# A transformer layer with routed experts: which batches are routed first, and who adds x for batch 0

## The chip, the cores and the metric

The kernel runs on one core of a Trainium2 chip. The metric is the device time of one execution in microseconds (us); less is better. A core has five engines that run side by side and meet at semaphores: TensorE (PE in the profile, PEld its weight loads), VectorE (DVE), ScalarE (ACT), GpSimd (POOL) and SyncE (SP), which here only issues DMAs. GpSimd issues the indirect DMAs, the ones whose rows are chosen by an index.

## What is computed

```python
def layer(x, ...):                                    # x: 4 batches x 512 tokens x 256, fp32
    x = x + layernorm(attention(layernorm(x)))        # 16 heads of 128, causal
    return x + layernorm(ffn(layernorm(x)))

def ffn(x):                                           # 2048 tokens
    logits = x @ router                               # 8 experts, each token goes to the best 2
    e, w = top2(logits); w = softmax(w)
    pos = rank of (token, choice) among those of its expert, in order of the tokens; kept if pos < 640
    buf[e, pos] = x[token]                            # the scatter
    out = (silu(buf @ gate) * (buf @ up)) @ down      # hidden width 176 per expert
    routed[token] += w * out[e, pos]                  # the gather
    shared = (silu(x @ sgate) * (x @ sup)) @ sdown    # hidden width 704
    return routed + shared
```

## The kernel before

Tokens stand in 16 tiles of 128 (TILES), four to a batch (TPB = 4, B = 4). Each engine has its own instruction stream, written out by hand; an engine runs its stream strictly in order, and every meeting between engines is a semaphore wait in the code. So the order of the lines in each engine's block is the schedule.

**Attention**, up to about 570 us, is a pipeline over 64 (batch, head) units. Batches 0 to 2 get their first norm, their sum with x and their second norm inside this pipeline. For batch 3 these come behind it: VectorE takes the projections back (`take_back`), normalizes them, adds x (line 1481) and takes the statistics of the sum (`stats_of_x2`, `variances`); GpSimd forms the inverse deviation (`inverse_std2`, line 1668); VectorE forms the shift (`scale_x2`); ScalarE writes the normalized tiles xn2 (`x_normed`, line 634); TensorE transposes them (`turn`, line 940).

**Routing** is done in two groups (GROUPS): group 0 is batches 0 to 2, twelve tiles, group 1 is batch 3, four tiles. For a group TensorE forms the logits (`logits`), ScalarE copies them (`logits_copied`), TensorE transposes them so that tokens stand on partitions (`turn_logits`, line 956), VectorE picks the experts (`choose`, lines 1410 to 1433), TensorE counts the positions (`positions`, lines 965 and 966), and VectorE turns them into row numbers (`find_slots`, lines 1442 to 1456; line 1454 writes at_in and frees `slots_ready`). GpSimd then issues two indirect DMAs a tile, 24 for group 0 and 8 for group 1, which scatter xn2 into slot_inputs in DRAM (line 1719).

**Shared expert, first part**: TensorE fills its time here with the first 384 of the 704 hidden columns: `shared_up(j)` (36 matmuls for a batch, line 1027, recorded at line 387), ScalarE's `silus`, VectorE's `shared_hidden` (line 1464), `shared_down(j)` (24 matmuls, line 1041), and ScalarE's `first_sum` (line 733), which takes the result out of PSUM banks 6 and 7. The routing of both groups is woven between these pieces.

**Experts**, about 640 to 728 us: SyncE waits for all 32 scatters, then loads xg (the slots of an expert, line 482). TensorE transposes them (`turn_slots`, line 1079), ScalarE and VectorE split them in a high and a low part, then come up, silu, product and down for each of the 8 experts in turn; the outputs go to slot_outputs.

**Tail**: TensorE does the second part of the shared expert (`shared_up`, `shared_down` for j = 4 to 7). Meanwhile GpSimd gathers 32 times 128 rows (line 1755). VectorE adds them with their weights (`routed_sum(pair)`, four instructions at line 1558 for two tiles, so two calls and eight instructions a batch), adds the shared part (`shared_sum`, line 1471) and takes statistics (`piece_stats`, `piece_scale`); ScalarE normalizes (line 792); x is added by GpSimd for batches 0 to 2 (line 1763) and by VectorE for batch 3 (line 1591); SyncE stores (line 516). Batch 3 is normalized in two halves.

## Time and profile before

| what | value |
|---|---|
| median of 3 runs | 800.16 us (797.98 to 803.86) |
| profiled execution, its own time | 799.27 us |
| its span, first to last instruction | 797.5 us |
| mean granted TensorE clock | 0.986 |
| busy: PE / DVE / ACT / POOL | 746.4 / 593.1 / 496.8 / 564.6 us |

The span is 1.8 us shorter than the time of its own execution; all times below are counted from the start of the span. A timeline row gives the start and the length of an instruction, or of several that are merged (x4), and in square brackets how long the engine had stood idle before it and what ended that. A busy TensorE has its matmuls overlapping: rows may add up to more than the time between them.

### The profile page before, as it was taken

The page shows a single profiled execution, that of the slowest core. Times are in us where ns is not written, and L with a number is a line of the kernel's source. Part 1 is how long each engine was busy: PE and PEld are TensorE (multiplying, and loading weights), DVE is VectorE, ACT ScalarE, POOL GpSimd, SP SyncE. Part 2 cuts the span into 40 slices and gives each one's busy share as a digit, 9 for nine tenths or more (in the row PEclk, how much of TensorE's full clock was granted, in tenths as well). Part 3 has the DMA queues.
Part 4 walks back from the last instruction along what each step waited for, and adds up shares of the span by engine and source line. Part 5 has one row for each costly group of instructions (what it writes and reads, how often), then busy time and mean ns, then how long its engine had stood idle before and what let it go on. Part 6 is the DMA issues. An engine that isn't in the chain of part 4 may idle for free.

```text
span 797.5 us, 13984 instructions
## 1 busy us (share of the span) xinstructions
PE 746.4 (94%) x4340; PEld 626.9 (79%) x4340; DVE 593.1 (74%) x1544; ACT 496.8 (62%) x1165; POOL 564.6 (71%) x473
## 2 busy tenths in 40 slices
PE   4899999999999999999999999999899779999993
PEld 4677787888888888888888888887687678898762
DVE  6648787787988887988887888888582147775467
ACT  5778776777776767676767676766542245653342
POOL 4767898888888887888887888885127734342775
PEclk9999999999999999999999999999999979999997
DMA  9311155431222122222221222220232235541333
GB/s 310 120 42 53 59 170 169 139 98 58 77 59 76 59 75 61 73 59 73 63 74 60 73 61 74 58 76 28 73 88 106 98 112 197 196 144 74 96 96 119
DMA packets 47733, 75.74 MB, mean 95 GB/s; under 512 B 9712, under 2 KB 24624, under 8 KB 47664
## 3 DMA queue, kind: packets, MB, share of 16 engines
q1 hardware_dynamic: 43504, 65.19, 26.0%
q0 software_dynamic: 3072, 8.39, 3.3%
q10 hardware_dynamic: 1088, 1.31, 0.5%
q8 instruction: 34, 0.56, 0.3%
q14 instruction: 35, 0.29, 0.1%
HBM read 57.71 MB, written 17.17 MB: 94 GB/s over the span
## 4 chain that ended last, share of the span: by engine, by line
PE 75%; DVE 7%; POOL 6%; ACT 5%; issue 4%; DMA 2%; DVEq 0%; ACTq 0%; POOLq 0%
PE ps L387 21%; PE ps L912 16%; PE ps L877 14%; PE ps L928 10%; PE ps L898 8%; PE ps L1041 4%; POOL slot_inputs L1719 1%; POOL o_lo L1656 1%; POOL kh_row L1651 1%; POOL q_lo L1646 1%; POOL q_sw L1642 1%; POOL q_sw L1634 1%; DVE hid_both L1536 1%; ACT prob L598 1%; DVE hid_hi L1526 1%
## 5 line engine op out<-in xcount | busy, mean ns | idle before, releaser
L598 ACT ACTIVATE prob<-ps,neg_max 128x512 f32<-128x512 f32 (+3 forms) x256 | 132.6, 527 | 74.5 <-DVE neg_max L1228 74.5
L912 PE MATMUL ps<-pt,vp 128*128 128x512 f32 (+3 forms) x512 | 149.0, 434 | 2.0 <-DVE pt L1241 1.6
L912 PEld LDWEIGHTS ps<-pt,vp 128*128 128x128 f32 x512 | 82.6, 190 | 50.4 <-DVE pt L1241 17.1
L1228 DVE CUSTOM_DVE_ANT_0 ps<-ps,causal_row 128x512 f32<-128x512 f32 (+3 forms) x256 | 117.4, 520 | 0.0
L1656 POOL TENSOR_TENSOR o_lo<-o_t,o_hi 128x512 fp32r<-128x512 f32 x64 | 85.8, 1341 | 42.3 <-ACT o_hi L626 42.2
L1646 POOL TENSOR_TENSOR q_lo<-q_sw,q_hi 128x512 fp32r<-128x512 f32 x62 | 83.5, 1346 | 41.7 <-ACT q_hi L620 41.7
L898 PE MATMUL ps<-id_f,prob 128*128 128x128 f32 x640 | 92.3, 275 | 3.9 <-ACT pt L607 3.9
L1241 DVE TENSOR_SCALAR pt<-ps,vcol 128x384 f32<-128x384 f32 (+2 forms) x192 | 82.6, 476 | 7.7 <-PE ps L898 7.7
L877 PE MATMUL ps<-k_hi,q_hi 128*128 128x512 f32 x248 | 87.1, 351 | 0.0
L1642 POOL TENSOR_TENSOR q_sw<-q_cos,q_sw 128x512 f32<-128x512 f32 x62 | 78.8, 1271 | 8.9
L1634 POOL TENSOR_TENSOR q_sw<-q_sw,rope_sb 128x512 f32<-128x512 f32 x64 | 82.1, 1282 | 3.0 <-ACT q_sw L587 2.9
L898 PEld LDWEIGHTS ps<-id_f,prob 128*128 128x128 f32 x640 | 72.6, 141 | 13.1 <-issue 5.0
L1651 POOL TENSOR_TENSOR kh_row<-kt,kh_row 128x512 f32<-128x512 f32 x62 | 82.6, 1332 | 0.0
L877 PE MATMUL ps<-k_lo,q_hi 128*128 128x512 f32 x248 | 80.4, 324 | 0.0
L877 PE MATMUL ps<-k_hi,q_lo 128*128 128x512 f32 x248 | 80.2, 323 | 0.0
L1220 DVE TENSOR_TENSOR q_cos<-ps,rope_sb 128x512 f32<-128x512 f32 x64 | 44.1, 689 | 48.2 <-ACT q_sw L587 48.0
L1247 DVE TENSOR_TENSOR k_lo<-kh_row,k_hi 128x512 fp32r<-128x512 f32 x62 | 73.7, 1189 | 0.0
L586 ACT COPY q_sw<-ps 64x512 f32<-64x512 f32 x64 | 37.3, 583 | 44.4 <-PE ps L387 43.7
L387 PE MATMUL ps<-xt_hi,wq_hi 128*128 128x512 f32 x128 | 51.4, 401 | 3.7 <-issue 2.5
L1255 DVE TENSOR_TENSOR o_t<-ps,inv_row 128x512 f32<-128x512 f32 x64 | 44.2, 691 | 13.6 <-PE ps L912 13.0
L928 PE MATMUL ps<-wo_hi,o_hi 128*128 128x256 f32 x256 | 52.6, 327 | 0.0
L598 ACT ACTIVATION_READ_ACCUMULATOR prob<-ps,neg_max 128x1 f32 x256 | 51.5, 201 | 0.0
(214 smaller groups left out, 1922.7 us busy)
## 6 DMA issues: line engine op xcount, KB each, us to landing
kh_row<-kvh_rows SPq DMA_DIRECT2D x64, 256.0 KB, 3.2
inv_row<-inverse_sums SPq DMA_DIRECT2D x64, 256.0 KB, 3.1
slot_inputs<-zeros SPq DMA_DIRECT2D x8, 640.0 KB, 4.8
xg<-slot_inputs SPq DMA_DIRECT2D x8, 640.0 KB, 4.5
slot_outputs<-yo SPq DMA_DIRECT2D x8, 640.0 KB, 3.3
up_raw<-in_w_up_dram SPq DMA_DIRECT2D x8, 368.0 KB, 4.6
wo_raw<-in_wout_dram SPq DMA_DIRECT2D x4, 512.0 KB, 7.8
dn_sb<-in_w_dn_dram SPq DMA_DIRECT2D x8, 256.0 KB, 3.6
```

The costliest lines, as they stand in the source:

```text
L387: last = pe.matmul(psum, w(o), m(o), start=(o == 0 and j == 0), stop=(o == EO - 1 and j == 2))
L598: ins = act.activation(prob[:, i % 2, ROW_AT[nt]:ROW_AT[nt] + w], ps_s[bank][:, at:at + w], ACT.Exp, scale=-1.0, bias=neg_max[:, i % 2, nt ...
L877: ins = pe.matmul(ps_s[bank][:, at:at + w], q_[:, r, qs], k_[:, r, 0:w], start=(nt == tiles[0] and j == 0), stop=(nt == tiles[-1] and j == ...
L898: ins = pe.transpose(ps_pt[bank][:, dst:dst + P], prob[:, i % 2, src:src + P], id_f[:])
L912: ins = pe.matmul(ps_qo[:, mt * P:SEQ], vp[:, b * TPB + mt, :], pt[:, i % 2, cols], start=(mt == 0), stop=(mt == PT_BANKS[-1][-1]))
L928: ins = pe.matmul(ps_acc[t // 2][:, at:at + E], o_[:, r, t * P:(t + 1) * P], w[:, h, :], start=(h == 0 and j == 0 and t % 2 == 0), stop=(h ...
L1228: ins = dve.tensor_tensor_reduce(s_, s_, causal_row[:, (NT - 1 - nt) * P:], 1.0, BIG, ALU.add, ALU.min, neg_max[:, i % 2, nt:nt + 1])
L1634: pool.tensor_tensor(q_sw[:], q_sw[:], sin_sb, ALU.mult).then_inc(q_sin_ready, 1)
L1642: pool.tensor_tensor(q_sw[:], q_cos[:], q_sw[:], ALU.add).then_inc(q_sum_ready, 1)
L1646: pool.tensor_tensor(q_lo[:, i % 2, :], q_sw[:], q_hi[:, i % 2, :].bitcast(F32), ALU.subtract) \
L1651: pool.tensor_tensor(kh_row[:, i % 2, :], kt[:, tok(batch(i))], kh_row[:, i % 2, :], ALU.mult) \
L1656: pool.tensor_tensor(o_lo[:, i % 2, :], o_t[:], o_hi[:, i % 2, :].bitcast(F32), ALU.subtract) \
```

## The change

On TensorE the transposed logits of group 0 come behind 12 instead of 24 matmuls of `shared_up(0)`, and the positions of group 0 straight behind `shared_up(0)`, so 24 matmuls earlier in all. The transposes of batch 3 move behind `shared_down(0)`, and `shared_down(1)` moves up from behind `positions(1)` to in front of `logits(1)`. On VectorE `choose(0)` and `find_slots(0)` move ahead of the sum with x and the second statistics of batch 3. On ScalarE `x_normed(3)` moves behind all of `silus(0)` and `silus(1)`, and both first sums go ahead of the logits of group 1. On GpSimd the second `inverse_std2` of batch 3 moves behind the fourth scatter. In the tail, VectorE adds x for batch 0 (in front of the hidden products of j = 7), GpSimd keeps batches 1 and 2, the store of batch 0 waits for VectorE, and the first routed sum of batch 3 goes ahead of the statistics of batch 2.

```diff
             for t0, t1 in LAST_LN:
                 b = t0 // TPB
-                if b < B - 1:
-                    sp.wait_ge(out_ready["pool"], t1)
+                if 0 < b < B - 1:
+                    sp.wait_ge(out_ready["pool"], t1 - TPB)
                 else:
-                    sp.wait_ge(out_ready["dve"], t1 - (B - 1) * TPB)
+                    sp.wait_ge(out_ready["dve"], t1 if b == 0 else t1 - (B - 2) * TPB)
...
             logits_copied(0)
-            silus(0, [0, 1])
+            silus(0)
+            silus(1)
             x_normed(B - 1)
-            silus(0, range(2, SH))
-            silus(1)
+            first_sum(0)
             turned_head(B - 1)
-            first_sum(0)
+            first_sum(1)
             logits_copied(1)
             silus(2)
-            first_sum(1)
             silus(3)
...
-                    if j == 1 and half == 1:
+                    if j == 2 and half == 1:
                         pe.wait_ge(pos_taken, 2)
...
             shared_up(0, [0])
-            pe.wait_ge(logit_copied, 1)
-            shared_up(0, [1])
             pe.wait_ge(y_taken, 2 * B)
             turn_logits(0)
-            shared_up(0, range(2, SH))
-            shared_up(1, [0, 1])
+            shared_up(0, range(1, SH))
             positions(0)
-            shared_up(1, range(2, SH))
+            shared_up(1)
             pe.wait_ge(sdn_in, 16 * len(RUNS))
             pe.wait_ge(pos_taken, 1)
             pe.wait_ge(s_hid_ready, SH + 1)
+            shared_down(0)
             turn(B - 1)
-            shared_down(0)
-            pe.wait_ge(sy_taken, 1)
+            shared_down(1)
+            pe.wait_ge(sy_taken, 3)
             logits(1)
             shared_up(2, [0])
-            pe.wait_ge(sy_taken, 2)
+            pe.wait_ge(sy_taken, 4)
             turn_logits(1)
             shared_up(2, range(1, SH))
             positions(1)
-            shared_down(1)
             shared_up(3)
...
                 normalize_y(B - 1, t)
+            choose(0)
+            shared_hidden(0, [0, 1])
+            find_slots(0)
+            shared_hidden(0, range(2, SH))
             dve.wait_ge(y_n_ready, TPB * B)
...
             variances(B - 1)
-            shared_hidden(0, [0, 1])
+            shared_hidden(1, [0, 1])
             scale_x2(B - 1)
-            choose(0)
-            shared_hidden(0, range(2, SH))
-            shared_hidden(1, [0])
-            find_slots(0)
-            shared_hidden(1, range(1, SH))
+            shared_hidden(1, range(2, SH))
             rest_of_turned(B - 1)
...
                 shared_sum(B + b)
+                if b == B - 2:
+                    routed_sum(2 * (B - 1))
                 piece_stats(b)
                 piece_scale(b)
-            for half in range(2):
-                routed_sum(2 * (B - 1) + half)
+                if b == 1:
+                    add_x(0, TPB)
+            routed_sum(2 * B - 1)
...
             inverse_std2(B - 1, 0)
-            inverse_std2(B - 1, 1)
...
                 for t in range(ts.start, ts.stop):
+                    if t == 2:
+                        inverse_std2(B - 1, 1)
                     for k in range(2):
...
-            for t in range((B - 1) * TPB):
+            for t in range(TPB, (B - 1) * TPB):
                 pool.wait_ge(out_normed, t + 1)
```

VectorE behind attention, before. y_back is batch 3's projection, x_sb the residual, s_hid the shared expert's hidden product, logit to counts is `choose(0)`, pos_sb begins `find_slots(0)`.

```order
L1297 TENSOR_SCALAR y_back<-y_back,mv,rstd 128x256 x4
L1481 TENSOR_TENSOR x_sb<-x_sb,y_back 128x1024
L1277 BN_STATS stats<-x_sb 128x6 x4
L1282 BN_AGGR mv<-stats 128x2 x4
L1288 TENSOR_SCALAR var_eps<-mv 128x4
L1464 TENSOR_TENSOR s_hid<-s_sg,ps 128x512 x2
L1305 SCALAR_TENSOR_TENSOR shift<-mv,rstd 128x4
L1410 COPY logit<-ps 128x4x3x8
L1412 MAX top<-logit 128x8 x12
L1415 MAX_INDEX top_at<-top,logit 128x8 x12
L1417 TENSOR_TENSOR gap<-top 128x12
```

The same place now; the lines are those of the changed file.

```order
L1293 TENSOR_SCALAR y_back<-y_back,mv,rstd 128x256 x4
L1406 COPY logit<-ps 128x4x3x8
L1408 MAX top<-logit 128x8 x12
L1411 MAX_INDEX top_at<-top,logit 128x8 x12
L1413 TENSOR_TENSOR gap<-top 128x12
L1416 CAST top_f<-top_at 128x96
L1419 TENSOR_TENSOR oh<-iota_sb,top_f 128x96 x2
L1422 TENSOR_TENSOR chosen_151<-oh 128x12x8
L1423 SCALAR_TENSOR_TENSOR counts_153<-same_expert,chosen_151 128x96
L1460 TENSOR_TENSOR s_hid<-s_sg,ps 128x512 x2
L1438 COPY pos_sb<-ps 128x8x12
```

The batch 3 part stands behind `find_slots(0)` now (at_in are the row numbers that the scatters wait for):

```order
L1450 TENSOR_SCALAR at_in<-slot_in 128x2x12
L1451 TENSOR_SCALAR pos<-pos 128x2x12
L1452 SCALAR_TENSOR_TENSOR at_out<-top_f,pos 128x2x12
L1460 TENSOR_TENSOR s_hid<-s_sg,ps 128x512
L1481 TENSOR_TENSOR x_sb<-x_sb,y_back 128x1024
L1273 BN_STATS stats<-x_sb 128x6 x4
L1278 BN_AGGR mv<-stats 128x2 x4
L1284 TENSOR_SCALAR var_eps<-mv 128x4
L1460 TENSOR_TENSOR s_hid<-s_sg,ps 128x512 x2
L1301 SCALAR_TENSOR_TENSOR shift<-mv,rstd 128x4
```

The sum with x and the statistics of batch 3 changed places with the choice and the slots of batches 0 to 2.

GpSimd from the end of attention to the first expert's weights, before:

```order
L1646 TENSOR_TENSOR q_lo<-q_sw,q_hi 128x512
L1656 TENSOR_TENSOR o_lo<-o_t,o_hi 128x512 x4
L1668 TENSOR_TENSOR rstd<-var_eps,neg_half 128x4 x2
L1719 DMA slot_inputs<-xn_91,at_in 5120x256 x32
L1728 CAST w_hi<-up_raw 128x736
```

And now:

```order
L1658 TENSOR_TENSOR o_lo<-o_t,o_hi 128x512 x4
L1670 TENSOR_TENSOR rstd<-var_eps,neg_half 128x4
L1720 DMA slot_inputs<-xn_91,at_in 5120x256 x4
L1670 TENSOR_TENSOR rstd<-var_eps,neg_half 128x4
L1720 DMA slot_inputs<-xn_91,at_in 5120x256 x28
L1729 CAST w_hi<-up_raw 128x736
```

The second inverse deviation now stands inside the row of scatters, behind four of them.

VectorE in the tail, from the hidden products of batch 3 on, before (got are the gathered rows):

```order
L1464 TENSOR_TENSOR s_hid<-s_sg,ps 128x512 x2
L1464 TENSOR_TENSOR s_hid<-s_sg,ps 64x512
L1558 SCALAR_TENSOR_TENSOR y_sb<-got,cw,y_sb 128x256 x8
L1471 TENSOR_TENSOR y_sb<-ps,y_sb 128x512 x2
L1277 BN_STATS stats<-y_sb 128x6 x4
L1282 BN_AGGR mv<-stats 128x2 x4
L1571 RECIPROCAL rstd<-std 128x4
L1305 SCALAR_TENSOR_TENSOR out_shift<-mv,rstd 128x4
L1558 SCALAR_TENSOR_TENSOR y_sb<-got,cw,y_sb 128x256 x8
L1471 TENSOR_TENSOR y_sb<-ps,y_sb 128x512
```

And now:

```order
L1574 TENSOR_TENSOR y_sb<-x_sb,y_sb 128x256 x4
L1460 TENSOR_TENSOR s_hid<-s_sg,ps 128x512 x2
L1460 TENSOR_TENSOR s_hid<-s_sg,ps 64x512
L1554 SCALAR_TENSOR_TENSOR y_sb<-got,cw,y_sb 128x256 x8
L1467 TENSOR_TENSOR y_sb<-ps,y_sb 128x512 x2
L1554 SCALAR_TENSOR_TENSOR y_sb<-got,cw,y_sb 128x256 x4
L1273 BN_STATS stats<-y_sb 128x6 x4
L1278 BN_AGGR mv<-stats 128x2 x4
L1567 RECIPROCAL rstd<-std 128x4
L1301 SCALAR_TENSOR_TENSOR out_shift<-mv,rstd 128x4
L1554 SCALAR_TENSOR_TENSOR y_sb<-got,cw,y_sb 128x256 x4
L1467 TENSOR_TENSOR y_sb<-ps,y_sb 128x512
```

Four additions of x are new on VectorE ahead of the hidden products, and batch 3's eight routed additions are split, four on either side of the statistics of batch 2.

## Rows read from the trace of the kernel before

**Rows 1.** The chain that ended last: start, length (us), what.

```profile
633.89 2.43 DMA slot_inputs<-xn,at_in
...
644.01 5.04 PE ps L387 x18
...
656.89 2.68 PE ps L387 x18
```

**Rows 2.** Timeline of GpSimd between attention and the experts.

```profile
583.36 1.01 POOL L1668 TENSOR_TENSOR rstd<-var_eps,neg_half 128x4 f32<-128x4 f32 x1 [4.92 <-DVE var_eps L1288]
594.00 1.24 POOL L1719 DMA_INDIRECT slot_inputs<-xn,at_in  x1 [9.63 <-issue]
...
633.89 0.97 POOL L1719 DMA_INDIRECT slot_inputs<-xn,at_in  x1 [0.30 <-issue]
```

**Rows 3.** Timeline of TensorE, single rows.

```profile
36.51 0.47 PE L387 MATMUL ps<-xt_hi,wq_hi 128*128 128x512 f32 x1 [2.52 <-issue]
...
558.76 1.57 PE L912 MATMUL ps<-pt,vp 128*128 128x384 f32 x6 [1.59 <-DVE pt L1241]
...
576.59 0.39 PE L387 MATMUL ps<-xt_hi,w_hi 128*128 128x512 f32 x1
...
582.04 0.50 PE L956 MATMUL ps<-id_f,logit_rows 96*128 96x96 f32 x4
...
590.67 0.21 PE L966 MATMUL ps<-counts,ones_b 128*128 128x96 bf16 x1
...
594.40 5.35 PE L1041 MATMUL ps<-sdn_sb,s_hid 128*128 128x256 f32 x24
...
640.48 1.94 PE L1079 MATMUL ps<-id_f,xg 128*128 128x128 f32 x8 [6.62 <-DMA xg<-slot_inputs]
```

**Rows 4.** Timeline of VectorE between attention and the experts, single rows.

```profile
579.90 1.22 DVE L1481 TENSOR_TENSOR x_sb<-x_sb,y_back 128x1024 f32<-128x1024 f32 x1
...
584.48 0.25 DVE L1410 COPY logit<-ps 128x96 f32<-128x96 f32 x1
...
588.90 0.36 DVE L1427 TENSOR_TENSOR_SCAN counts<-same_expert,chosen 128x96 bf16<-128x96 bf16 x1
...
590.91 0.35 DVE L1442 COPY pos_sb<-ps 128x96 f32<-128x96 f32 x1 [0.48 <-PE ps L966]
...
592.79 0.18 DVE L1454 TENSOR_SCALAR at_in<-slot_in 128x24 uint32<-128x24 f32 x1
...
612.10 0.17 DVE L1454 TENSOR_SCALAR at_in<-slot_in 128x8 uint32<-128x8 f32 x1
```

**Rows 5.** Stretches: us, busy of each engine (x instructions), granted clock, DMA share, GB/s.

```profile
34.00:37.70 3.70, 1.19 (x5) 1.04 (x6) 3.70 (x12) 3.67 (x11) 3.34 (x4) 1.00 0.00 0
37.80:41.00 3.20, 3.03 (x8) 2.04 (x7) 1.30 (x3) 2.93 (x7) 3.07 (x3) 0.50 0.30 84
...
554.00:560.00 6.00, 3.98 (x24) 2.62 (x22) 5.02 (x7) 3.20 (x7) 1.27 (x1) 1.00 0.01 2
...
638.60:648.60 10.00, 6.96 (x27) 6.59 (x28) 2.64 (x6) 3.17 (x5) 1.45 (x1) 0.50 0.55 207
```

**Rows 6.** Timeline of the tail, GpSimd and VectorE.

```profile
746.88 1.82 POOL L1755 DMA_INDIRECT got<-slot_outputs,at_out  x1 [0.30 <-DVE y_sb L1558]
...
778.37 9.35 POOL L1763 TENSOR_TENSOR y_sb<-x_sb,y_sb 128x256 f32<-128x256 f32 x12
...
772.39 2.01 DVE L1464 TENSOR_TENSOR s_hid<-s_sg,ps 128x512 f32<-128x512 f32 x3 [4.06 <-ACT s_sg L646]
774.32 3.54 DVE L1558 SCALAR_TENSOR_TENSOR y_sb<-got,cw,y_sb 128x256 f32<-128x256 f32 x8
...
779.35 1.41 DVE L1277 BATCH_NORM_STATS2 stats<-y_sb 128x6 f32<-128x256 f32 x4
...
781.82 6.58 DVE L1558 SCALAR_TENSOR_TENSOR y_sb<-got,cw,y_sb 128x256 f32<-128x256 f32 x8
788.43 0.69 DVE L1471 TENSOR_TENSOR y_sb<-ps,y_sb 128x512 f32<-128x512 f32 x1
```

More of the change, by code:

```diff
@@ L1572, in piece_scale, with add_x @@
                 shift_of(ts, out_shift)
+            def add_x(t0, t1):
+                for t in range(t0, t1):
+                    dve.wait_ge(out_normed, t + 1)
+                    dve.tensor_tensor(y_sb[:, t, :], x_sb[:, t, :], y_sb[:, t, :], ALU.add).then_inc(out_ready["dve"], 1)
             shared_hidden(B)
@@ L1588, in _ @@
                 piece_scale(B - 1 + half)
-            for t in range((B - 1) * TPB, TILES):
-                dve.wait_ge(out_normed, t + 1)
-                dve.tensor_tensor(y_sb[:, t, :], x_sb[:, t, :], y_sb[:, t, :], ALU.add).then_inc(out_ready["dve"], 1)
+            add_x((B - 1) * TPB, TILES)
         @block.gpsimd
```

## The prediction, written before the changed kernel ran

> **What bounds the kernel now.** I read the chain that ended last first. Through attention it is TensorE, and the change touches nothing there. From 633.89 us it runs over the last scatter: 2.43 us of its DMA, the load of xg, then TensorE's transposes and the first expert [rows 1]. Next comes GpSimd's timeline there: its first scatter starts at 594.00 and the 32nd at 633.89, one after the other, each 0.97 us with 0.30 us ahead of it [rows 2]. That is 39.89 us for 31 steps, 1.29 a step. So GpSimd is the bound of this stage from the moment it may start. TensorE's row says the same from the other side: it stands idle for 6.62 us up to 640.48, waiting for xg [rows 3]; its own shared work was over at 633.86. Group 1 is not late: its row numbers are there at 612.27 [rows 4], when GpSimd is still busy with group 0 (24 scatters from 594.00 end near 624.9). What sets the stage is when at_in of group 0 is written, 592.97 [rows 4], 1.03 us ahead of the first scatter [rows 2]. The experts and TensorE's tail behind it are shifted as a whole by whatever this stage gives.
>
> In the tail I read the timelines of VectorE and GpSimd. GpSimd adds x for twelve tiles from 778.37 for 9.35 us, and meanwhile VectorE's eight routed additions take 6.58 us, against 3.54 for the same eight a little earlier [rows 6]. The last shared sums come behind them, at 788.43, so that stretch is on the end's path.
>
> **Part 1: the start of the scatters.** On TensorE `shared_up(0)` starts at 576.59 and the transposed logits come at 582.04 behind 24 matmuls, 0.227 us each [rows 3]. Behind twelve they come at 576.59 + 12 x 0.227 = 579.3 and are ready at 579.8. VectorE is free at 579.90, where it now begins the sum with x [rows 4]; there `choose(0)` begins instead. From 584.48 to the end of its last row, 589.26, it takes 4.78 us [rows 4]: done at 584.7. TensorE reaches the positions after 24 more matmuls, at 585.2, so it does not wait, but by half a microsecond only. VectorE does two hidden products (three take 2.01, so 1.3 [rows 6]) until 585.9, and the counts are ready by then. `find_slots(0)` thus begins at 585.9 instead of 590.91: 5.0 us earlier. At_in follows 2.06 us later, the first scatter starts at 589.0.
>
> **Part 2: what is now inside the row of scatters.** The second `inverse_std2` costs 1.01 us [rows 2]. Bounds for putting it between scatters: 1.0, and 1.6, where the next scatter pays its 0.30 and is as long as the first one (1.24 against 0.97). I take 1.3, between them. It also waits for VectorE: var_eps came 3.4 us behind the start of the sum with x (579.90 to 583.36 [rows 2, 4]). That sum now starts behind `find_slots(0)` and one hidden product, near 588.9, so var_eps is there at 592.3. GpSimd gets to it after four scatters, at 594.1. Nothing is waited for, with 1.8 us in hand; behind this wait stand 28 scatters, so every microsecond past that would be paid in full. VectorE's busier stretch under the first scatters may cost a little: a gather beside its routed additions was 1.82 instead of 1.0 once [rows 6]. I take 0.2, with 0 and 0.8 as ends. Part 1 and 2: -5.0 + 1.3 + 0.2 = -3.5; the last scatter starts at 630.4 and xg frees TensorE at 637.0.
>
> **Part 3: is group 1 in time?** Batch 3's shift comes when the inverse deviation is there, near 595.3, and its four tiles (ScalarE, some 2.1 us) by 597.4. TensorE, which did the same matmuls in another order, is at the end of `shared_down(0)` at 593.5 + 5.2 = 598.7 (a `shared_down` is 5.35 [rows 3]) and goes on without a wait. One more `shared_down` ahead of `logits(1)` puts everything of group 1 back by about 5: row numbers at 617.2 instead of 612.27. GpSimd needs them at 589.0 + 24 x 1.28 + 1.5 = 621.2. Four microseconds in hand, cost nothing. TensorE still ends its shared work near 633.9; what would make it wait must reach 3.1 us before it replaces the scatters as the bound, since xg is there at 637.0.
>
> **Part 4: TensorE's clock.** The granted clock was 0.50 from 638.6 to 648.6 [rows 5], the 1.2 GHz level. It had fallen 4.7 us after the last matmul and stayed low through the first expert's start: 18 matmuls took 5.04 us, and 2.68 at full clock later [rows 1]. With eight transposes (1.94 [rows 3], about half of that at full clock) 3.1 to 3.3 us hang on it. The idle stretch shrinks from 6.62 to about 3.1. Does the clock hold then? Two gaps of this trace bound it. After 1.59 us idle at 558.76 it stayed at 1.00; after 2.52 us idle ahead of 36.51 it was at 0.50 from 37.8 on, with 1.2 us of matmuls between [rows 3, 5]. A gap of 3.1 is nearer to, and longer than, the one that cost it. So I expect it to fall again, but beginning sooner relative to the transposes, and to be back sooner. Ends: 0 and -3.3; I take -1.0.
>
> **Part 5: the tail.** VectorE's four additions for batch 0 take 4 x 0.42 = 1.7 us and lie in the 4.06 us that it stood idle before the hidden products [rows 6]; cost nothing there. They may lengthen a gather or two beside them by the 0.8 seen; the gathers have slack, since the last one's rows are wanted five microseconds later. GpSimd's row of additions shrinks from twelve to eight, 9.35 to 6.2 us, and four of these wait for batch 2's normalized tiles. Of VectorE's eight routed additions four run from 779.3 while GpSimd adds batch 1, until about 781.6: contended they cost 0.82 each (6.58 / 8), alone 0.44 (3.54 / 8). That is 2.9 us. The statistics follow, 2.5 us (779.35 to 781.82 [rows 6]), to 784.7. The other four run half against batch 2's additions: 2.5 us, to 787.2, where it was 788.43 before. That is -1.2. Ends: 0, if all stay contended, and -3.0, if none is (8 x 0.38 less).
>
> The SBUF — State Buffer page of the Trainium skill, section "Who interferes with whom", says that a VectorE instruction with two SBUF inputs contends with a GpSimd instruction that reads SBUF, and that the loser blocks for the whole of the other. The trace agrees in kind: 6.58 against 3.54 us for eight [rows 6]. By that rule VectorE's new additions for batch 0 speak against the change too, for they have two SBUF inputs and run beside gathers; by the sole row with such an excess that is 0.8 us on GpSimd, which has slack.
>
> **Sum.** -3.5 - 1.0 - 1.2 = -5.7 us. Against the profiled execution's own time, 799.27, that is 793.6. The median of the three runs lies 0.9 above that execution, and the changed kernel will be a median too, so I put 794.4, 0.7% below 800.16. A measurement of this kernel can tell about 1% from no change.
>
> **Rivals.**
> 1. *The clock holds.* Then part 4 is -3.3 instead of -1.0, total -8.0, about 792.1, just 1% faster. For it: the gap is less than half of before, and with 6.62 us of it the clock had most of that time to fall. Against: the fall after 2.52 us at 36.51.
> 2. *The head start is eaten.* The inverse deviation waits for var_eps on GpSimd, or TensorE waits for `choose(0)` (only 0.5 us in hand), or the scatters run slower beside VectorE. Two microseconds of that leave -1.5 of part 1 and 2, and with -0.5 of the clock and -1.2 of the tail -3.2: about 796.9. For it: three margins of 0.5, 1.8 and 3.1 us on estimates. Against: each is met by the rows.
> 3. *Slower: batch 3's transposes come too late.* They now stand on TensorE behind an inverse deviation that stands behind four scatters on GpSimd, which in turn wait for all of group 0's choice. Whatever they come late stops TensorE at `turn(3)`, and with it `shared_down(1)`, the logits of group 1 and all that follows. Up to 3.1 us it is hidden by the scatters; from there TensorE's own end replaces them, at 6.6 us it has eaten parts 1 and 2, and with the 2.2 of clock and tail the kernel is slower from 8.8 us on. A wait of 12 us there would give 794.4 + 12 - 3.1 = 803.3. For it: the chain of four engines is new. Against: the tiles are there 1.3 us ahead by the rows above.
>
> **How the numbers follow.** Forecast 0.55, rival 1 0.23, rival 2 0.17, rival 3 0.05. Low end: rival 1 with the tail's best end, -3.8 - 3.3 - 2.5, near 790.5. High end: rival 2 with no gain from clock or tail, 798.5. Faster by over 1% (under 792.2): half of rival 1 and a fifth of the forecast, 0.24. Slower by over 1%: 0.03, from rival 3. The rest, 0.73, lies within 1%.
>
> **What would show each step.** Part 1: at_in of group 0 near 588 and the first scatter near 589. Part 2: 28 scatters without a gap behind one 1.0 us row; a gap before that row says var_eps was late. Part 3: no idle of TensorE between 572 and 634, and no pause between the 24th and 25th scatter. Part 4: TensorE idle about 3 us ahead of the transposes, then the clock in the next ten. Part 5: GpSimd with eight additions, the last-but-one shared sum about 9 us before the end as now, and four plus four routed additions under 5.6 us in sum. The forecast is wrong if the first scatter starts later than 591, or if the span from xg's landing to the end is not shorter.

## The result and the profile after

The changed kernel takes 794.60 us, median of 5 runs (793.21 to 794.79), against 799.54 us (797.98 to 803.86, 5 runs) before: ratio 0.9924, 95% interval 0.9897 to 0.9951. That is 0.8% faster by the ratio and 4.9 us by the medians, inside the 1% that the prediction called no change. The profiled execution took 794.79 us, span 792.9, against 799.27 and 797.5. In the three later sets of runs, from which the experiments come, the kernel before took 798.53, 798.60 and 798.57 us (17, 16 and 29 runs), 1.0 us less than in this one. The changed kernel was timed in this set alone. So where a kernel below is set against its 794.60 us, a difference of about a microsecond is not settled by the times, and I go by the profiles.

GpSimd's timeline after (start, length, idle before; the first, second and fourth scatter, the inverse deviation, the fifth scatter, the 25th, which is the first of group 1, and the last):

```profile
588.83 2.12 POOL L1720 DMA_INDIRECT slot_inputs<-xn,at_in  x1 [10.36 <-issue]
591.26 0.99 POOL L1720 DMA_INDIRECT slot_inputs<-xn,at_in  x1 [0.31 <-issue]
...
593.83 0.97 POOL L1720 DMA_INDIRECT slot_inputs<-xn,at_in  x1 [0.31 <-issue]
594.82 1.06 POOL L1670 TENSOR_TENSOR rstd<-var_eps,neg_half 128x4 f32<-128x4 f32 x1
596.07 1.04 POOL L1720 DMA_INDIRECT slot_inputs<-xn,at_in  x1 [0.19 <-issue]
...
621.71 0.97 POOL L1720 DMA_INDIRECT slot_inputs<-xn,at_in  x1 [0.30 <-issue]
...
630.65 0.97 POOL L1720 DMA_INDIRECT slot_inputs<-xn,at_in  x1 [0.30 <-issue]
```

The first scatter starts 5.17 us earlier than in [rows 2], the last one 3.24. The 1.93 us that are lost in between stand here. The inverse deviation makes the step from the fourth to the fifth scatter 2.24 us (593.83 to 596.07) instead of 1.28, and the fifth is 0.07 us longer, together 1.03. The first scatter takes 2.12 instead of 1.24 us, 0.88 more.

VectorE's timeline after, the places that answer to [rows 4]:

```profile
579.88 0.26 DVE L1406 COPY logit<-ps 128x96 f32<-128x96 f32 x1
...
585.76 0.33 DVE L1438 COPY pos_sb<-ps 128x96 f32<-128x96 f32 x1
...
587.62 0.18 DVE L1450 TENSOR_SCALAR at_in<-slot_in 128x24 uint32<-128x24 f32 x1
...
588.63 1.22 DVE L1481 TENSOR_TENSOR x_sb<-x_sb,y_back 128x1024 f32<-128x1024 f32 x1
...
617.27 0.30 DVE L1450 TENSOR_SCALAR at_in<-slot_in 128x8 uint32<-128x8 f32 x1
```

The choice starts 4.6 us earlier, the counts are read 5.15 us earlier, and VectorE waits for nothing in between. Group 1's row numbers are there at 617.57, 5.3 us later than before. GpSimd asks for them when the 24th scatter is issued, at 621.40 (0.30 us ahead of the 25th), and has to wait for nothing.

TensorE after, and its clock (columns as in [rows 3] and [rows 5]):

```profile
637.19 1.07 PE L1075 MATMUL ps<-id_f,xg 128*128 128x128 f32 x8 [3.37 <-DMA xg<-slot_inputs]
```

```profile
634.00:638.40 4.40, 1.21 (x10) 1.07 (x10) 0.00 (x0) 0.99 (x3) 2.74 (x3) 1.00 0.86 298
638.60:645.20 6.60, 5.12 (x19) 5.13 (x20) 2.88 (x6) 2.33 (x4) 0.00 (x0) 0.51 0.50 159
645.40:650.00 4.60, 4.60 (x37) 4.59 (x36) 3.81 (x8) 3.54 (x9) 1.83 (x3) 0.99 0.00 0
```

It stands idle for 3.37 us instead of 6.62, and between 572 and 634 not at all. The clock falls again, for 6.8 us instead of 10. The transposes now still run at full clock (1.07 us instead of 1.94), the 18 matmuls behind them do not.

The tail after (VectorE and GpSimd; GpSimd has 4 + 4 additions):

```profile
764.48 1.43 DVE L1574 TENSOR_TENSOR y_sb<-x_sb,y_sb 128x256 f32<-128x256 f32 x4
...
774.82 3.15 POOL L1764 TENSOR_TENSOR y_sb<-x_sb,y_sb 128x256 f32<-128x256 f32 x4
775.46 3.20 DVE L1554 SCALAR_TENSOR_TENSOR y_sb<-got,cw,y_sb 128x256 f32<-128x256 f32 x4
...
781.16 2.67 DVE L1554 SCALAR_TENSOR_TENSOR y_sb<-got,cw,y_sb 128x256 f32<-128x256 f32 x4
...
781.96 3.13 POOL L1764 TENSOR_TENSOR y_sb<-x_sb,y_sb 128x256 f32<-128x256 f32 x4 [3.99 <-ACT y_sb L791]
783.86 0.69 DVE L1467 TENSOR_TENSOR y_sb<-ps,y_sb 128x512 f32<-128x512 f32 x1
```

The first four routed additions run wholly beside four of GpSimd's, the second four for the most part (from 781.96 on), and they take 3.20 and 2.67 us; alone four take 1.7 (1.66 in two_batches below).

To see where each kernel below gains, I read three marks from its profile: TensorE's first transposes of xg, VectorE's split of the second shared weights (w_hi from sw_raw, right behind the last expert), and the last-but-one shared sum on VectorE (line 1471 before). Between the first and the second lie the experts, and with them the price of the clock; between the second and the third lies the tail. One more mark divides the experts: "first hid" is the time from xg to TensorE's first down matmul (line 1106 before), which waits for VectorE's first hidden product, and "rest" is the time from there to the split. The slow clock lies in the first of these two columns.

| kernel | first scatter | xg | split | sum | xg to split | first hid | rest | split to sum |
|---|---|---|---|---|---|---|---|---|
| before | 594.00 | 640.48 | 728.56 | 788.43 | 88.1 | 14.3 | 73.7 | 59.9 |
| changed | 588.83 | 637.19 | 724.79 | 783.86 | 87.6 | 13.8 | 73.8 | 59.1 |
| routing_only | 588.69 | 637.01 | 723.83 | 783.73 | 86.8 | 13.7 | 73.2 | 59.9 |
| tail_only | 593.95 | 640.47 | 728.56 | 787.61 | 88.1 | 14.5 | 73.6 | 59.1 |
| filler | 588.45 | 639.33 | 724.06 | 783.12 | 84.7 | 11.6 | 73.1 | 59.1 |
| before_filler | 593.60 | 645.82 | 730.52 | 791.43 | 84.7 | 11.6 | 73.1 | 60.9 |
| filler_7 | 588.46 | 636.80 | 722.20 | 781.24 | 85.4 | 11.7 | 73.7 | 59.0 |
| before_filler_14 | 594.48 | 640.83 | 727.67 | 787.56 | 86.8 | 13.1 | 73.7 | 59.9 |
| two_batches | 588.42 | 636.80 | 724.49 | 782.01 | 87.7 | 14.0 | 73.7 | 57.5 |
| turn_first | 589.35 | 640.87 | 725.61 | 784.69 | 84.7 | 11.6 | 73.1 | 59.1 |
| pow_8 | 588.56 | 639.90 | 724.60 | 783.67 | 84.7 | 11.6 | 73.1 | 59.1 |
| no_routed_split | 589.73 | 638.21 | 726.31 | 784.76 | 88.1 | 14.5 | 73.6 | 58.5 |
| x_later | 589.08 | 636.54 | 723.38 | 782.45 | 86.8 | 13.8 | 73.1 | 59.1 |
| best | 588.62 | 636.89 | 722.24 | 779.76 | 85.4 | 11.7 | 73.7 | 57.5 |

The starts of the spans differ by some tenths from one execution to the next, so the last four columns say more than the marks themselves. The "rest" column has two values, 73.1 to 73.2 and 73.6 to 73.8, and the clock is not the reason: it was granted at 1.00 over "rest" in every profile. First the row that ends "first hid", in the kernel before, in the changed one and in filler:

```profile
654.82 0.39 PE L1106 MATMUL ps<-dn_hi,hid_hi 128*128 128x256 f32 x1 [0.86 <-DVE hid_both L1536]
...
651.03 0.39 PE L1102 MATMUL ps<-dn_hi,hid_hi 128*128 128x256 f32 x1 [0.70 <-DVE hid_both L1532]
...
650.93 0.39 PE L1102 MATMUL ps<-dn_hi,hid_hi 128*128 128x256 f32 x1 [0.94 <-DVE hid_both L1534]
```

Then the fourth expert on VectorE and GpSimd, in the changed kernel (hid_both is a hidden product of this expert, w_hi the cast of another one's weights):

```profile
682.15 1.09 DVE L1532 TENSOR_TENSOR hid_both<-hid,hid_both 48x320 fp32r<-48x320 f32 x1
682.10 0.80 POOL L1729 CAST w_hi<-up_raw 128x736 fp32r<-128x736 f32 x1 [1.57 <-DMA up_raw<-in_w_up_dram]
```

The same place in routing_only, whose rest is 73.2:

```profile
681.80 0.48 DVE L1532 TENSOR_TENSOR hid_both<-hid,hid_both 48x320 fp32r<-48x320 f32 x1
681.89 1.06 POOL L1726 CAST w_hi<-up_raw 128x736 fp32r<-128x736 f32 x1 [1.71 <-DMA up_raw<-in_w_up_dram]
```

Where GpSimd's cast begins first, VectorE's instruction takes 1.09 instead of 0.48 us and TensorE waits for it; where VectorE begins first, the cast takes 1.06 instead of 0.80 and TensorE loses nothing. Each of the eight profiles with 73.6 or more has one such long hid_both (0.97 to 1.12 us, behind the start of a cast by 0.2 us or less) that the six with 73.1 or 73.2 do not have, in the fourth expert or in the sixth; five others of 0.91 to 0.97 us stand in all fourteen. So 0.5 to 0.7 us of the column "xg to split" hang on a meeting that a shift of 0.1 to 0.2 us makes or avoids.

### The profile page after: what moved, and what is told of

Read it like the earlier page. It is cut to its first block, busy times and chain, and to the rows that moved or that the text cites. A ratio compares the mean times of both kernels' runs of the same rounds, so it can differ in the third digit from the quotient of the medians.

```text
span 792.9 us, 13984 instructions
## 1 busy us (share of the span) xinstructions
PE 745.7 (94%) x4340; PEld 626.4 (79%) x4340; DVE 593.1 (75%) x1548; ACT 496.7 (63%) x1165; POOL 562.5 (71%) x469
## 4 chain that ended last, share of the span: by engine, by line
PE 75%; DVE 7%; POOL 5%; ACT 5%; issue 4%; DMA 2%; DVEq 0%; ACTq 0%; POOLq 0%
PE ps L387 22%; PE ps L911 16%; PE ps L876 14%; PE ps L927 10%; PE ps L897 8%; PE ps L1040 4%; POOL o_lo L1658 1%; POOL kh_row L1653 1%; POOL q_lo L1648 1%; POOL q_sw L1644 1%; POOL q_sw L1636 1%; DVE hid_both L1532 1%; ACT prob L598 1%; DVE hid_hi L1522 1%; DVE hid L1527 1%
## 5 line engine op out<-in xcount | busy, mean ns | idle before, releaser
L1243 DVE TENSOR_TENSOR k_lo<-kh_row,k_hi 128x512 fp32r<-128x512 f32 x62 | 73.6, 1187 | 0.0
L1251 DVE TENSOR_TENSOR o_t<-ps,inv_row 128x512 f32<-128x512 f32 x64 | 44.2, 691 | 13.7 <-PE ps L911 13.0
```

## The experiments

### The two halves of the change

`routing_only` is the changed kernel with the old tail, `tail_only` the old kernel with the new tail:

```diff
# routing_only, against the changed kernel
-                if b == B - 2:
-                    routed_sum(2 * (B - 1))
...
-                if b == 1:
-                    add_x(0, TPB)
...
-            for t in range(TPB, (B - 1) * TPB):
+            for t in range((B - 1) * TPB):
                 pool.wait_ge(out_normed, t + 1)
```

The store's waits, not shown, go with them.

> The changed kernel with the whole tail of the kernel before (GpSimd adds x for batches 0 to 2, the routed sums of batch 3 together); only the routing half of the change is left. My theory by the two traces: xg reaches TensorE 3.3 us earlier and the experts' end is 3.8 us earlier, the tail gives 0.8. So 3.8 us under the kernel before, near 795.6, ratio 0.9952, and the last-but-one shared sum 3.8 us earlier than at 788.43. Rival (the tail carries most of it): under 2 us.

> The kernel before with only the tail half of the change. Theory: 0.8 us under the kernel before (near 798.8), first scatter at 594.0 as before, last-but-one shared sum near 787.6 instead of 788.43. Rival: the two halves are not additive, the tail alone gives 2 us or more (no contention left when GpSimd has eight additions) or nothing.

Measured: routing_only 795.16 us, ratio to the kernel before 0.9956 (0.9940 to 0.9971); tail_only 797.75, ratio 0.9983 (0.9972 to 0.9995). The kernel before took 798.53 in that comparison. So the routing carries about 0.44% (3.4 us by the medians) and the tail 0.17% (0.8 us by the medians and by the marks). The tail's column is 59.9 with the old tail and 59.1 with the new one, whatever the routing. The medians of the halves add up to 4.2 us, where the whole change showed 4.9 against a kernel before that was 1.0 us slower. The profile of routing_only alone shows more, 4.7 us at the last-but-one shared sum: the long hid_both, 0.6 us, is not in it, and the slow clock took 0.2 us less than in the changed kernel's profile; so the halves add within what single profiles can tell. The rival of a tail that carries most is out.

### The price of the clock

Matmuls whose result nobody reads fill TensorE's idle time ahead of the experts:

```diff
             pe.wait_ge(s_hid_ready, B * SH)
+            for _ in range(14):                 # 29 in before_filler
+                pe.matmul(ps[3][:, 0:E], s_hid[0:P, 1, 0, 0:P], sdn_sb[0:P, 0, 0, :], start=True, stop=True)
             turn_slots(0, 0)
```

> The changed kernel with 14 matmuls of 256 columns (3.0 us, results thrown away, into a free PSUM bank) between TensorE's last shared matmul and the first expert's transposes, so that its 3.4 us of idle time are filled. Theory (the clock is what the short idle still costs): granted clock 1.00 from 634 to 650, the 18 matmuls of the first up product 2.7 us instead of 5.2, the time 2.5 us under the changed kernel's 794.6, near 792.1. Rival (the start of the experts is bound by something else, xg_hi, xg_lo or the weights): clock at 1.00 and under 1 us gained.

> The kernel before with 29 such matmuls (6.2 us) in its 6.6 us of idle time. Theory: clock 1.00 there, 3.1 to 3.3 us under the kernel before, near 796.4, which measures the whole price of the clock that the prediction put at 3.1 to 3.3. If so, of that the change itself gave back 0.5 to 0.8 us. Rival as for the other filler: under 1 us gained.

Measured: filler 793.97 us, 0.9944 (0.9930 to 0.9958); before_filler 802.99, 1.0054 (1.0038 to 1.0069). The fill was twice as long as I meant. The trace writes two records for each of these fp32 matmuls, so its 24 rows of a `shared_down` are 12 matmuls in the code, of 0.43 us each:

```profile
633.28 6.21 PE L1123 MATMUL ps<-sdn_sb,s_hid 128*128 128x256 f32 x28
```

TensorE was thus held past xg's landing, by about 2.5 and 5.7 us (its transposes start 9.05 and 12.33 us behind the last scatter's start, where the kernels without a fill take 6.5 to 6.6). From the transposes on both kernels show what was asked: the clock is at 1.00, and the experts take 84.7 us, not 88.1. But not all of this 3.4 us is the clock: 0.6 is the long hid_both, which the fill happens to avoid. The column "first hid" holds the clock's part: 11.6 us at full clock, 14.3 in the kernel before and 14.5 in tail_only. So the price before the change is 2.7 to 2.9 us, against 3.1 to 3.3 in the prediction. It was 2.2 us in the changed kernel's profiled execution, and 2.1, 2.4 and 2.9 in those of routing_only, two_batches and no_routed_split, which have nearly the same idle stretch. filler as a whole gained 0.6 us on the changed kernel's median, not the 2.5 expected, since its transposes come late. before_filler's tail took 60.9 us, 1.0 more than any other: GpSimd's twelve additions stand 1.3 us later behind the split than in the kernel before and so beside more of VectorE's instructions. Its shift of batch 2 took 0.72 instead of 0.16 us and its eight routed additions 7.07 instead of 6.58. Then with half as many:

> As the filler with 14 matmuls, but with 7: there each took 0.43 us and not the 0.215 that I had reckoned with, so that the fill was 6.2 us long and held TensorE 2.3 us beyond xg's landing. Seven are 3.0 us and fit into the 3.4 us of idle time. Theory (the clock costs the changed kernel what 14 showed from the transposes on, 87.6 us to the last expert's end against 84.7): 2.1 to 2.9 us under the changed kernel, near 792.0. Rival: the clock falls all the same, or nothing is gained.

> The kernel before with 14 of these matmuls, 6.0 us of its 6.6 idle. Theory: 84.7 us from the first expert's transposes to the last expert's end instead of 88.1, so 3.4 us under the kernel before, near 795.1, which is nearly what the whole change gives.

filler_7: 792.34 us, 0.9917 (0.9902 to 0.9932) of the kernel before (798.60 there). By the medians that is 2.3 us under the changed kernel, as expected, and by the ratios only 0.07%, within the intervals; the profiled executions are 2.6 us apart, 2.1 of them in "first hid". Its clock, in a row over the first expert:

```profile
636.80:650.00 13.20, 10.63 (x78) 10.19 (x79) 9.29 (x18) 7.33 (x16) 4.35 (x4) 1.00 0.27 99
```

before_filler_14: 796.62, 0.9973 (0.9961 to 0.9985), 2.0 us faster than before and not 3.4. Of the 3.4 only 2.7 were the clock. The profiled execution (798.41, the second slowest of ten) shows that the clock fell all the same:

```profile
634.00:640.00 6.00, 6.00 (x30) 5.23 (x28) 0.00 (x0) 0.59 (x1) 5.53 (x6) 1.00 0.49 156
640.00:642.00 2.00, 1.50 (x12) 1.08 (x10) 0.00 (x0) 0.48 (x1) 0.56 (x1) 1.00 0.77 317
...
645.00:646.00 1.00, 1.00 (x5) 1.00 (x5) 0.00 (x0) 0.44 (x1) 0.00 (x0) 0.50 0.97 397
```

Here TensorE idled for 0.50 us ahead of the transposes and 1.60 behind them, waiting for xg's low parts, and yet the clock fell for some three microseconds. In filler_7 the same two waits, 0.34 and 1.6 us, left it at 1.00. "First hid" is 13.1 us there, so that 1.5 us of the price were left. So what the clock costs at this place differs between executions and kernels with nearly the same gaps, and single profiles do not settle it to better than a microsecond.

### The tail's two edits

> The changed kernel with batch 3's eight routed additions together behind the statistics of batch 2, as before; VectorE still adds x for batch 0. Theory (GpSimd's additions of batch 1 then fall on the statistics, which read one SBUF input and are not slowed): six of the eight routed additions meet an idle GpSimd or batch 2's additions only, so the last-but-one shared sum comes 58.3 us behind the split of the second shared weights, against 59.1 now: 0.7 us faster than the changed kernel. Rival (the split is what gave the tail's 0.8 us): 59.9, as in the kernel before.

```diff
-                if b == B - 2:
-                    routed_sum(2 * (B - 1))
...
-            routed_sum(2 * B - 1)
+            for half in range(2):
+                routed_sum(2 * (B - 1) + half)
```

Its tail takes 58.5 us, against 59.1 with the split and 59.9 with neither edit. The eight additions and GpSimd's rows beside them:

```profile
779.54 5.18 DVE L1554 SCALAR_TENSOR_TENSOR y_sb<-got,cw,y_sb 128x256 f32<-128x256 f32 x8
```

```profile
776.32 2.77 POOL L1763 TENSOR_TENSOR y_sb<-x_sb,y_sb 128x256 f32<-128x256 f32 x4
780.34 3.32 POOL L1763 TENSOR_TENSOR y_sb<-x_sb,y_sb 128x256 f32<-128x256 f32 x4 [1.26 <-ACT y_sb L791]
```

They take 5.18 us, where the split pair took 3.20 + 2.67. GpSimd's additions for batch 1 fall on VectorE's statistics and are done before the routed additions begin. So x for batch 0 on VectorE gave 1.4 us and the split took 0.6 back; the split without it was not run. By its whole time, 794.94 us, 0.9952 (0.9936 to 0.9968), the kernel cannot be told from the changed one: in the profiled execution the experts took 88.1 us against 87.6, so the clock ("first hid" 14.5) hides a gain of this size.

> The changed kernel where VectorE adds x for batches 0 and 1, each straight behind its own piece_scale, in the two idle stretches (4.1 us each) ahead of the hidden products; GpSimd keeps batch 2 alone. Theory (VectorE's routed additions take 0.8 each only while GpSimd adds): the four of batch 3's first half take 1.9 us instead of 3.2, so 1.2 us under the changed kernel, and the last-but-one shared sum 57.9 us behind the split of the second shared weights instead of 59.1. Rival: VectorE's additions beside the gathers delay these or the hidden products, nothing or a loss.

```diff
-                if b == 1:
-                    add_x(0, TPB)
+                if b < B - 2:
+                    add_x(b * TPB, (b + 1) * TPB)
...
-            for t in range(TPB, (B - 1) * TPB):
+            for t in range((B - 2) * TPB, (B - 1) * TPB):
```

The store's waits, not shown, change with it.

two_batches: 792.75 us, 0.9926 (0.9911 to 0.9940). The tail takes 57.5 us, 1.55 less than the changed kernel's, where 1.2 was expected. VectorE's timeline:

```profile
764.91 1.90 DVE L1574 TENSOR_TENSOR y_sb<-x_sb,y_sb 128x256 f32<-128x256 f32 x4 [0.67 <-ACT y_sb L791]
...
775.14 1.66 DVE L1554 SCALAR_TENSOR_TENSOR y_sb<-got,cw,y_sb 128x256 f32<-128x256 f32 x4
...
779.31 2.67 DVE L1554 SCALAR_TENSOR_TENSOR y_sb<-got,cw,y_sb 128x256 f32<-128x256 f32 x4
```

With GpSimd still, four routed additions take 1.66 instead of 3.20 us; the other four still meet batch 2's additions. The additions for x cost nothing in VectorE's idle stretches: from the split of the weights to batch 2's routed additions it is 45.7 us (770.23) as in the changed kernel, 45.8 (770.55). The first four gain because the other engine is quiet (GpSimd has no row between 774.48 and 780.11). Whether the split itself pays here is not shown: no run has x for two batches without it.

### Where batch 3 could be late

> The changed kernel with batch 3's transposes back in front of the first shared sums on TensorE (and ScalarE's turned_head in front of its first sums). Theory (the turn was put behind them to cover the wait for xn2): xn2 is there at 598.2 and TensorE would want it at 593.6, so it idles 4.6 us; its shared work ends at 638.4 instead of 633.8 and group 1's row numbers come at 622, 2 us behind the 24th scatter; xg about 2 us later, 795.5 to 796.5 if the clock goes as before. Rival (my slower rival has a smaller price): hidden, no change.

> The changed kernel with the second inverse deviation behind eight scatters instead of four. Theory (the chain GpSimd, VectorE, ScalarE, TensorE has 0.6 us in hand at the turn): xn2 5.1 us later, TensorE idles 4.5 us ahead of batch 3's transposes, group 1's row numbers near 622, the scatters pause for 2 us, xg 2 us later; TensorE's idle stretch ahead of the first expert nearly vanishes, which may save the clock there, but may lose it at 600. 794 to 797. It measures the point from which the slower rival decides.

```diff
# turn_first; ScalarE's turned_head(B - 1) goes ahead of first_sum(0) too
-            shared_down(0)
             turn(B - 1)
+            shared_down(0)
             shared_down(1)
# pow_8
-                    if t == 2:
+                    if t == 4:
                         inverse_std2(B - 1, 1)
```

turn_first: 795.51 us, 0.9958 (0.9942 to 0.9974); pow_8: 796.61, 0.9971 (0.9956 to 0.9987), its twelve runs from 793.38 to 799.77. Rows of turn_first on TensorE and on GpSimd:

```profile
598.87 1.94 PE L939 MATMUL ps<-id_f,xn 128*128 128x128 f32 x8 [4.58 <-ACT xn L634]
```

```profile
625.24 0.97 POOL L1720 DMA_INDIRECT slot_inputs<-xn,at_in  x1 [3.32 <-DVE at_in L1450]
```

TensorE idled 4.58 us, as worked out (4.43 in pow_8), and fell to half clock there. That made group 1's row numbers later than those 4.6 us: GpSimd stood idle for 3.32 us ahead of the 25th scatter, so the scatters paused for 3.0 us and not for 2. The span of turn_first starts 0.5 us earlier ahead of its work than the changed kernel's (GpSimd's first inverse deviation starts at 577.95 there, at 577.45 in the changed kernel, at 577.12 in pow_8). With that taken off, xg came 3.2 us later than in the changed kernel, 3.0 in pow_8, and there was no idle left ahead of it, so the experts took 84.7 us instead of 87.6: 2.2 us by the full clock, and 0.7 because the long hid_both did not occur. Nearly all of the loss came back that way in these two profiles: the split is 0.3 and 0.1 us late. The medians say more, 0.9 and 2.0 us above the changed kernel's. The profile of pow_8 is not typical of its runs: it is one of the three with a mean granted clock of 0.991 or more, which took 793.38 to 794.50 us, while the other nine stood at 0.985 to 0.989 and took 795.35 to 799.77. So its loss goes with the clock; where in the kernel the clock was low in those nine, no trace shows. So the cover that the change built for batch 3's transposes is needed, and the margin at the turn is the 0.6 us between 598.2, when ScalarE is done with xn2, and 598.8, when TensorE gets to it.

### The long first scatter

> The changed kernel with one hidden product of batch 1 (one input in PSUM) ahead of the sum with x on VectorE, so that the sum with x, 1.22 us with two SBUF inputs, starts 0.6 to 0.7 us later than the first scatter. Theory (the first scatter took 2.12 us instead of 1.24 because it met that instruction): the excess of 0.9 us gets smaller or moves to the second scatter. Rival (it is the first scatter's own start): 2.1 us again. Time within 0.5 us of the changed kernel.

```diff
+            shared_hidden(1, [0])
             dve.wait_ge(y_n_ready, TPB * B)
...
-            shared_hidden(1, [0, 1])
+            shared_hidden(1, [1])
```

x_later: 793.30 us, 0.9929 (0.9910 to 0.9947). GpSimd and VectorE:

```profile
589.08 1.24 POOL L1721 DMA_INDIRECT slot_inputs<-xn,at_in  x1 [10.37 <-issue]
590.62 0.99 POOL L1721 DMA_INDIRECT slot_inputs<-xn,at_in  x1 [0.31 <-issue]
```

```profile
588.28 1.27 DVE L1460 TENSOR_TENSOR s_hid<-s_sg,ps 128x512 f32<-128x512 f32 x2
589.47 1.22 DVE L1482 TENSOR_TENSOR x_sb<-x_sb,y_back 128x1024 f32<-128x1024 f32 x1
```

The first scatter is 1.24 us again, as in the kernel before, and no other one is longer. In the changed kernel the sum with x began at 588.63, 0.2 us ahead of the scatter, which then lasted 2.12 us; in eight other profiles with that order it did so too, 2.12 or 2.13 each. Here the sum begins 0.4 us behind the scatter's start and costs it nothing. So the order in which the two begin decides whether the scatter is long. The SBUF — State Buffer page of the Trainium skill, section "Who interferes with whom", states that VectorE with two SBUF inputs contends with a GpSimd instruction that reads SBUF, that the hold is exclusive, and that the order of issue decides who blocks. The trace agrees for two compute instructions, in both orders (hid_both and the cast, above). For the scatter it agrees one way only: the sum with x takes 1.22 us in x_later too, its length in the kernel before, though the scatter had begun first, so nothing held VectorE. The same section says that a `tensor_tensor` did not stall a DMA; here one made the issue of an indirect DMA 0.88 us longer, and the measurement decides. Which part of the scatter's issue is held is not shown. The 0.9 us is gone by one swapped product: from the first scatter to the last it is 40.93 us in x_later and 41.82 in the changed kernel. The median, 793.30, is 1.3 us under the changed kernel's and the ratios are alike (0.9929 and 0.9924), so the times do not settle it.

### The two best together

> Both together, seven filler matmuls and x for two batches on VectorE. Theory: the gains add, 3.5 to 4 us under the changed kernel, near 790.8; against the kernel before a ratio near 0.990.

best: 791.44 us (790.59 to 792.47), 0.9910 (0.9893 to 0.9927) of the kernel before. Its columns are those of its two parts, 85.4 and 57.5 us. The changed kernel stood at 0.9924 (0.9897 to 0.9951) in another comparison, so the lead over it is 3.2 us by the medians and 0.14% by the ratios, with intervals that overlap. Against its two parts, timed in the same set, it is 0.9 us (filler_7) and 1.3 us (two_batches) faster. The profiled executions are 4.2 us apart (790.59 and 794.79), where 3.5 to 4 was expected. The swap of x_later was not tried on top of it.

## Why the prediction was right

The forecast was 794.4 us, the median came to 794.60. The mechanism held: each term has the sign that was forecast, and that of the clock half the size. But the hit to 0.2 us is luck. The sum was -5.7 us; the spans differ by -4.6 and the profiled times by -4.5. So the terms were 1.1 us too hopeful, 0.2 in parts 1 and 2 (at the transposes), 0.5 in the clock and 0.4 in the tail. Against this stood the 0.9 us that I had set the median above the profiled sum, 793.6; the changed kernel's profiled execution, 794.79, lies 0.2 above its median and not 0.9 below. The two errors cancel. The forecast also started from a median of three, 800.16; five runs gave 799.54 and later sets 798.6, so the gain by the medians is 4.0 to 4.9 us and not the 5.8 of the forecast. One sum of the chances is off: half of rival 1 and a fifth of the forecast are 0.225 and not 0.24.

- **Part 1** put at_in at 588 and the first scatter at 589.0: 587.8 and 588.83. TensorE had no idle time there.
- **Part 2** took 1.3 us for the inverse deviation, and it was 1.03 (0.96 on the step, 0.07 on the next scatter; in x_later, too, the 31 steps take 1.04 more than before). VectorE's contention was mis-sized: I took 0.2, with 0.8 as the upper end, and it was 0.88, all on the first scatter. The term came to -5.17 + 1.03 + 0.88, -3.2 where -3.5 stood (-3.24 at the last scatter, -3.29 at the transposes).
- **Part 3** held: row numbers at 617.57 (617.2), wanted at 621.4 (621.2), no idle on TensorE. turn_first and pow_8 show what the slower rival costs: a wait of 4.4 to 4.6 us costs 0.1 to 0.3 us in the profiles and 1 to 2 us by the medians. My 6.6 us for eating parts 1 and 2 was too generous in one way, since the clock falls behind that wait and the scatters pause longer, and too strict in another, since the experts then start at full clock.
- **Part 4** said that the clock would fall again and be back sooner. It did, and -1.0 was -0.5 in the profiled execution ("first hid" 14.34 to 13.84), -0.7 in routing_only's (13.67) and nothing in no_routed_split's (14.47). The whole of it is 2.7 to 2.9 us and not 3.1 to 3.3. I had counted the faster transposes in full; TensorE then waits longer for xg's low parts, 1.60 instead of 1.16 us (filler against before), and the 18 matmuls start 2.9 us behind the transposes' start instead of 3.5. Rival 1 (the clock holds) did not happen in any profile without a fill ahead of the experts, except where TensorE came late (turn_first, pow_8) and had no idle stretch.
- **Part 5** gave -1.2 for the tail, and it was -0.8: the four additions beside batch 1's took 3.20 instead of 2.9, the other four 2.67 instead of 2.5. The step missed that the two edits work against each other: by the columns 59.9, 58.5 and 59.1 the first makes the tail 1.4 us shorter and the split then 0.6 longer.
- **Rival 2** is partly in the numbers (the longer first scatter), but no margin was broken.

## What to carry to other kernels

When one engine issues a row of DMAs back to back, read what starts that row, and pull it forward; an instruction put inside the row costs its full length (1.03 us for one of 1.06), and an instruction of a neighbour that begins just ahead of its first member can cost nearly as much (0.88). A stretch of idle time on TensorE that is shortened may still cost the slow clock behind it: from 6.62 to 3.37 us it gave back 0 to 0.8 of 2.7 to 2.9 us. Measure that price by filling the gap, and read it where the clock was low and not over the whole stage, since the fill shifts what lies behind: here 0.6 us of 3.4 was a chance meeting of two other engines. When work is moved between VectorE and GpSimd, compare the eight instructions' length alone and beside the other engine: here 0.42 against 0.8 us each.

## What the runs showed that I had not expected

- A delayed TensorE lost little in the profiles: turn_first and pow_8 brought xg 3.2 and 3.0 us later and were 0.3 and 0.1 us late at the split, because without idle time ahead of the experts these took 84.7 instead of 87.6 us.
- An instruction of 0.48 us on VectorE in the fourth or sixth expert decides over 0.5 to 0.7 us of the whole kernel, by whether GpSimd's cast begins before or after it.
- The clock fell for three microseconds in before_filler_14 after idle times of only 0.50 and 1.60 us with 1.1 us of transposes between them, and not in filler_7 with 0.34 and 1.6.
- An fp32 matmul of 256 columns takes 0.43 us and stands as two records in the trace. Where my text on the kernel says 24 matmuls for a `shared_down`, these are records; the code issues 12.
